# A graph layer on one core: the edge stage rebuilt, with 400 quads of 500 edges in place of 391 of 512

## The chip, the cores and the metric

The kernel runs on one core of a Trainium2 chip. The time is the device time of one execution in microseconds (us); the median of three runs of the kernel before is 2057.42 us (2057.03 to 2058.61).

## The reference

12500 nodes of 64 features, 200000 edges sorted by their destination `dst`. All is float32.

```python
h = jnp.maximum(_layernorm(x, axis=-1), 0.0)
e = jnp.concatenate([h[src], h[dst]], axis=1)
m = jax.nn.relu(e @ W1 + b1) @ W2 + b2            # 128 -> 128 -> 64
s = jax.ops.segment_sum(m, dst, num_segments=n_nodes)
cnt = jax.ops.segment_sum(jnp.ones((m.shape[0],)), dst, num_segments=n_nodes)
return x + s / jnp.maximum(cnt, 1.0)[:, None]
```

## The kernel before, in words

**Node stage.** The layer norm is worked out in ten groups of ten nodes for each of 125 partitions. PE multiplies h with the two halves of W1 (`products`, L815 to L819). The first half gives table P, the second, with b1 added by DVE (L659), table Q; both are stored in HBM by SP (L295, L296), in pieces of 112 and 13 partitions. So an edge needs relu(P[src] + Q[dst]).

**Edge tables.** `src` and `dst` are turned into columns by PE (L795): `src_e` holds the source of each edge as an integer, `rel_e` its destination less the smallest destination of its quad (L604).

**Edge stage.** A quad is 512 edges in four chunks of 128. There are 391 quads. As `dst` is sorted, the destinations of a quad lie in a window of 128 nodes if no quad's span is wider; `if_one_window` (L221) takes the branch `fast` then, as with this data. For quad n:

- ACT copies four columns of indices into `idx` (L484), nine quads ahead; POOL then issues four indirect DMAs, each of which fetches 128 rows of P into `g`, a ring of 12 quads (L388). The first 12 quads are gathered ahead of the loop.
- SP loads the window, 128 rows of Q, into `qw` (L307).
- DVE compares `rel_e` with the numbers 0 to 127, chunk by chunk: `member`, ones and zeros, edges by nodes (L675). ACT makes a bf16 copy (L514), PE transposes it (L894) and also counts with it (L899), ACT copies the transposes to `spread` (L490) and the counts to SBUF (L497).
- PE multiplies `spread` with the window (L874): Q[dst] of each edge. DVE adds the gathered rows (L685), ACT does the relu (L508).
- PE sums the edges of each node: `r` by `member` (L885). ACT copies the sums (L502), PE multiplies them with w2 and adds b2 times the counts (L905, L906), and DVE adds this to the window's columns of `acc` (L704) and the counts to `count` (L697).

The order on each engine is written out by hand: `quads(n)` works on different quads, PE's on the products of quad n-1, the sums of n-2, the transposes of n, the w2 product of n-3. `rounds` (L207) puts twelve such steps into a loop. Waits are on semaphores that count quads, with a credit of `RING` so that a value is never negative.

**Output.** SP fetches the counts laid out by node (L326), DVE takes their reciprocals (L709, L711). PE transposes `acc`, a node of each partition's hundred at a time (L975), and DVE (L785) or ACT and POOL (L573, L416) scale it and add x; SP stores. The 25 batches of four go through eight PSUM banks.

## Time and profile before

| | us |
|---|---|
| plain runs, median of 3 | 2057.4 |
| profiled execution, span from first to last instruction | 3104.2 |
| PE busy, matrix products | 1916.4 |
| POOL busy | 1516.6 |
| ACT busy | 884.8 |
| DVE busy | 866.9 |
| first gather starts at | 62.0 |
| output stage starts at | 3077.0 |

The profile is of one execution, and beside its span no separate time of that execution is given. Mind that the span is 1.5 times the plain runs. Busy time counts instructions that compute or generate descriptors; waiting isn't in it. PE's matrix products are pipelined, and a float32 product is recorded as two passes.

### The profile page before, as it was taken

How to read it: one execution, taken by the hardware profiler on the slowest of the kernel's cores; microseconds unless marked ns; L12 is line 12 of the kernel's file. 1: busy time of each engine (PE TensorE's matmuls, PEld its weight loads, DVE VectorE, ACT ScalarE, POOL GpSimd, SP SyncE). 2: the span in 40 equal slices, each digit the busy share in tenths (PEclk: the TensorE clock that was granted, in tenths of full speed). 3: DMA queues.
4: the chain of work that ended last, by engine and by line, in shares of the span. 5: the costliest groups of instructions: out<-in, count | busy, mean ns of one | idle time of the engine just before them, and what ended most of it. 6: DMA issues, size and time to landing. Idle time of an engine off the chain costs nothing.

```text
span 3104.2 us, 46493 instructions
## 1 busy us (share of the span) xinstructions
PE 1916.4 (62%) x11540; PEld 1632.1 (53%) x11541; DVE 866.9 (28%) x2889; ACT 884.8 (29%) x2458; POOL 1516.6 (49%) x1611
## 2 busy tenths in 40 slices
PE   6256555655655566765556665565655667665568
PEld 6255444545555555554445555454555556554457
DVE  6122222222222222222222222222222222222224
ACT  3123222322222222222222222222222222222224
POOL 5445444544545444454445444454545445454451
PEclk9577777777777776677777667777777766677778
DMA  6311111111111111111111111111111111111111
GB/s 183 92 52 46 43 44 43 43 43 44 44 43 45 43 43 43 44 45 43 44 43 46 43 44 43 43 45 44 44 44 44 44 43 44 44 44 44 44 44 43
DMA packets 112927, 150.93 MB, mean 49 GB/s; under 512 B 32653, under 2 KB 83212, under 8 KB 112750
## 3 DMA queue, kind: packets, MB, share of 16 engines
q0 software_dynamic: 50016, 102.53, 12.6%
q1 hardware_dynamic: 62170, 46.62, 5.1%
q14 instruction: 165, 1.35, 0.1%
q10 hardware_dynamic: 564, 0.23, 0.0%
q8 instruction: 12, 0.20, 0.0%
HBM read 133.09 MB, written 16.07 MB: 48 GB/s over the span
## 4 chain that ended last, share of the span: by engine, by line
another core or an unknown queue 41%; PE 28%; issue 14%; ACT 10%; DVE 4%; DVEq 2%; DMA 1%; ACTq 1%; SPq 0%; POOL 0%; PEldq 0%; POOLq 0%
PE bank L874 12%; PE bank L885 11%; ACT spread L490 4%; ACT member L514 3%; PE bank L894 2%; DVE z L685 2%; ACT spans_i L497 1%; DVEq L689 1%; PE bank L975 1%; PE bank L817 1%; ACT idx L484 1%; PE bank L905 1%; PE bank L899 0%; PE bank L906 0%
## 5 line engine op out<-in xcount | busy, mean ns | idle before, releaser
L388 POOL DMA_INDIRECT g<-p_table,idx x1563 | 1476.0, 944 | 1504.6 <-ACT idx L484 1022.8
L874 PE MATMUL bank<-qw,spread 128*128 128x128 f32 x3126 | 647.1, 371 | 1044.4 <-ACT spread L490 985.2
L874 PEld LDWEIGHTS bank<-qw,spread 128*128 128x128 f32 x3126 | 551.4, 265 | 1106.8 <-ACT spread L490 857.0
L490 ACT CAST spread<-bank 128x512 f32<-128x512 bf16 x391 | 228.7, 585 | 1713.2 <-remote 1335.2
L885 PE MATMUL bank<-member,r 128*128 128x128 f32 x3126 | 616.9, 360 | 63.3 <-DVE acc L704 42.5
L697 DVE TENSOR_TENSOR area<-area,spans_i 1x128 f32 x391 | 109.6, 280 | 1949.0 <-ACT spans_i L497 1773.9
L885 PEld LDWEIGHTS bank<-member,r 128*128 128x128 f32 x3126 | 544.8, 263 | 106.6 <-DVE acc L704 38.9
L675 DVE TENSOR_SCALAR member<-columns,rel_e 128x128 f32<-128x128 f32 x1563 | 349.2, 290 | 107.0 <-PE bank L885 85.2
L508 ACT ACTIVATE r<-z 128x512 f32<-128x512 f32 x391 | 246.1, 630 | 371.5 <-DVE z L685 279.5
L685 DVE TENSOR_TENSOR z<-bank,g 128x512 f32<-128x512 f32 x391 | 263.7, 674 | 0.0
L514 ACT CAST member<-member 128x512 bf16<-128x512 f32 x391 | 235.3, 602 | 4.3 <-DVE member L675 4.3
L905 PE MATMUL bank<-w 128*128 128x128 f32 x782 | 211.4, 356 | 0.0
L906 PE MATMUL bank<-spans_i,b_row 1*128 1x128 f32 x782 | 197.9, 334 | 0.0
L894 PE MATMUL bank<-ident,member 128*128 128x128 bf16 x1563 | 183.3, 251 | 5.1 <-issue 5.1
L899 PE MATMUL bank<-member,ones 128*1 128x128 bf16 x1563 | 172.9, 242 | 0.0
L905 PEld LDWEIGHTS bank<-w 128*128 128x128 f32 x782 | 131.6, 211 | 56.7 <-issue 23.6
L894 PEld LDWEIGHTS bank<-ident,member 128*128 128x128 bf16 x1563 | 149.2, 117 | 17.0 <-ACT member L514 5.3
L906 PEld LDWEIGHTS bank<-spans_i,b_row 1*128 1x128 f32 x782 | 120.7, 193 | 52.6 <-issue 11.9
L704 DVE TENSOR_TENSOR acc<-acc,bank 128x128 f32 x391 | 112.8, 289 | 81.5 <-issue 43.7
L899 PEld LDWEIGHTS bank<-member,ones 128*1 128x1 bf16 x1563 | 88.5, 88 | 52.2 <-issue 24.3
L497 ACT COPY spans_i<-bank 1x128 f32<-1x128 f32 x391 | 98.0, 251 | 4.2 <-remote 3.2
L502 ACT COPY w<-bank 128x128 f32<-128x128 f32 x391 | 97.5, 249 | 4.6 <-PE bank L885 4.6
(66 smaller groups left out, 434.8 us busy)
## 6 DMA issues: line engine op xcount, KB each, us to landing
qw<-q_table SPq DMA_DIRECT2D x391, 64.0 KB
g<-p_table,idx POOLq DMA_INDIRECT x1563
p_table<-area SPq DMA_DIRECT2D x10, 560.0 KB
q_table<-area SPq DMA_DIRECT2D x10, 560.0 KB
xs<-in_x_dram SPq DMA_DIRECT2D x5, 560.0 KB
out_dram<-xs SPq DMA_DIRECT2D x3, 672.0 KB
acc<-in_src_dram SPq DMA_DIRECT2D x1, 768.0 KB
acc<-in_dst_dram SPq DMA_DIRECT2D x1, 768.0 KB
```

The source lines that it names most:

```text
L388: nc.gpsimd.indirect_dma_start(out=g[:, k, j * HID:(j + 1) * HID], out_offset=None, in_=p_table, in_offset=bass.IndirectOffsetOnAxis(ap=id ...
L490: nc.scalar.copy(spread[:, k % 2, :, :].rearrange("p c e -> p (c e)")[:, 0:w], t_bank[k % 2][:, 0:w]).then_inc(spread_done, 1)
L508: nc.scalar.activation(r[:, k % 2, 0:w], z[:, k % 2, 0:w], ACT.Relu).then_inc(r_done, 1)
L514: nc.scalar.copy(member16[:, k % MEMBERS, 0:c, :], member[:, k % MEMBERS, 0:c, :]).then_inc(member16_done, 1)
L675: last = nc.vector.tensor_scalar(member[:, k % MEMBERS, j, :], columns[:, :], rel_e[:, bass.ds(n * 4 + j, 1)], None, ALU.is_equal)
L685: nc.vector.tensor_tensor(z[:, k % 2, 0:w], z_bank[k % 2][:, 0:w], g[:, k, 0:w], ALU.add).then_inc(z_done, 1)
L874: last = nc.tensor.matmul(z_bank[k % 2][:, HID * j:HID * (j + 1)], spread[:, k % 2, j, :], qw[:, k, :], start=True, stop=True)
L885: last = nc.tensor.matmul(sums[:, 0:WIN], r[:, k % 2, HID * c:HID * (c + 1)], member[:, k % MEMBERS, c, :], start=c == 0, stop=c == chunks ...
L894: last = nc.tensor.transpose(t_bank[k % 2][:, 128 * c:128 * (c + 1)], member16[:, k % MEMBERS, c, :], ident16[:, :])
L899: last = nc.tensor.matmul(c_bank[k % 2][0:1, 0:WIN], ones16[:, :], member16[:, k % MEMBERS, c, :], start=c == 0, stop=c == chunks_of(n) - 1)
L905: nc.tensor.matmul(u_bank[k][:, 2 * WIN:3 * WIN], w2[:, :], of_sums, start=True, stop=False)
L906: return nc.tensor.matmul(u_bank[k][:, 2 * WIN:3 * WIN], b2_row[:, :], of_counts, start=False, stop=True)
```

## The change

- A quad is 500 edges, four chunks of 125; there are 400 quads, none partly filled. 1600 gathers of 125 rows replace 1563 of 128. They read their indices from `src_e`; `idx` is gone. The ring has 16 quads, the windows a ring of their own of 8.
- The transposed membership is made in another way: `rel_q` holds the relative destinations of a quad in one row, as bf16 (values over 255 cut to 255). PE spreads that row over 128 partitions with a product (`broadcast_rows`), and DVE compares it with each partition's number (`spread_of`). `member` is made by one comparison of the quad; the counts use its upper halves as bf16.
- The sum z and its relu are written in place in `g`.
- What is added to `acc` is the sum of the relu rows, straight from PSUM, and the counts too. The products with w2 and b2 are made at the end for all nodes, in place of the transposes of `acc`.
- The loops are written out without `Fori`.

The diff, cut to its core:

```diff
-QE = 512
+ROWS = 125
+QE = 4 * ROWS
-RING = 12
+RING = 16
+WINDOWS = 8
+FAR = 255.0
-MEMBERS = 4
+MEMBERS = 3
...
+        def ones_and_zeros(k, c):
+            return member[0:ROWS, k, c, :].bitcast(BF16).rearrange("e (w h) -> e w h", h=2)[:, :, 1]
...
             def fast():
-                rounds(sp, 0, QUADS, load_window)
+                for n in range(QUADS):
+                    k = n % WINDOWS
+                    if n >= WINDOWS:
+                        sp.wait_ge(zq_done, n - WINDOWS + 1)
+                    at = sp.value_load(base_i[0:1, n:n + 1], min_val=0, max_val=NODES - 1)
+                    sp.dma_start(qw[:, k, :], q_table[bass.ds(at, WIN), :]).then_inc(window_in[k], 16)
...
-            def gather(n, k, use):
-                ready = pool.to_reg(n + 1)
-                pool.wait_ge(p_out[0], all_out[0])
-                pool.wait_ge(idx_ready, ready)
+            pool.wait_ge(src_table, QT)
+            def gather(n):
+                k = n % RING
+                if n >= RING:
+                    pool.wait_ge(u_psum, n - RING + 1)
                 for j in range(chunks_of(n)):
                     nc.gpsimd.indirect_dma_start(
-                        out=g[:, k, j * HID:(j + 1) * HID], out_offset=None, in_=p_table,
-                        in_offset=bass.IndirectOffsetOnAxis(ap=idx[:, k, j:j + 1], axis=0)).then_inc(gathered[k], 16)
+                        out=g[0:ROWS, k, j * HID:(j + 1) * HID], out_offset=None, in_=p_table,
+                        in_offset=bass.IndirectOffsetOnAxis(ap=src_e[0:ROWS, 4 * n + j:4 * n + j + 1], axis=0))\
+                        .then_inc(gathered[k], 16)
...
             def fast():
-                for n in range(LAG):
-                    quads(n, n, 0)
-                rounds(act, LAG, QUADS - LEAD, quads)
...
+                for n in range(QUADS):
+                    w = HID * chunks_of(n)
+                    act.wait_ge(z_done, n + 1)
+                    nc.scalar.activation(g[0:ROWS, n % RING, 0:w], g[0:ROWS, n % RING, 0:w], ACT.Relu)\
+                        .then_inc(r_done, 1)
...
+            def rows_of():
+                dve.wait_ge(low_done, 1)
+                for t in range(QT):
+                    nc.vector.tensor_scalar(rel_q[:, t, :], dst_f[:, t, :], low[:, t:t + 1], FAR,
+                                            ALU.subtract, ALU.min).then_inc(row_table, 1)
...
+            def spread_of(n):
+                w = ROWS * chunks_of(n)
+                dve.wait_ge(row_done, n + 1)
+                if n >= 2:
+                    dve.wait_ge(zq_done, n - 1)
+                nc.vector.tensor_scalar(spread[:, n % 2, 0:w], row_bank[n % 2][:, 0:w], rows_f[:, :], None,
+                                        ALU.is_equal).then_inc(spread_done, 1)
+            def members_of(n):
+                if n >= MEMBERS:
+                    dve.wait_ge(u_psum, n - MEMBERS + 1)
+                nc.vector.tensor_tensor(member[0:ROWS, n % MEMBERS, :, :],
+                                        columns[0:ROWS, :].unsqueeze(1).to_broadcast([ROWS, 4, WIN]),
+                                        rel_e[0:ROWS, 4 * n:4 * n + 4].unsqueeze(2).to_broadcast([ROWS, 4, WIN]),
+                                        ALU.is_equal).then_inc(member_done, 1)
+            def add_rows(n):
                 w = HID * chunks_of(n)
+                rows_n = g[0:ROWS, n % RING, 0:w]
+                dve.wait_ge(zq_done, n + 1)
+                dve.wait_ge(gathered[n % RING], n // RING * 64 + 16 * chunks_of(n))
+                nc.vector.tensor_tensor(rows_n, z_bank[n % 2][0:ROWS, 0:w], rows_n, ALU.add).then_inc(z_done, 1)
+            def add_sums(n):
+                at = dve.value_load(base_i[0:1, n:n + 1], min_val=0, max_val=NODES - 1)
+                v, c = acc[:, bass.ds(at, WIN)], count[:, bass.ds(at, WIN)]
+                dve.wait_ge(u_psum, n + 1)
...
+                nc.vector.tensor_tensor(v, v, u_bank[n % 2][:, 0:WIN], ALU.add).then_inc(v_done, 1)
...
+                nc.vector.tensor_tensor(c, c, u_bank[n % 2][0:1, WIN:2 * WIN], ALU.add).then_inc(c_done, 1)
...
+                for n in range(QUADS + 2):
+                    if n + 1 < QUADS:
+                        spread_of(n + 1)
+                    if n < QUADS:
+                        add_rows(n)
+                    if n + 1 < QUADS:
+                        members_of(n + 1)
+                    if n >= 2:
+                        add_sums(n - 2)
...
+            def broadcast_rows(n):
+                w = ROWS * chunks_of(n)
+                if n >= 2:
+                    pe.wait_ge(spread_done, n - 1)
+                nc.tensor.matmul(row_bank[n % 2][:, 0:w], ident16[:, n % 128:n % 128 + 1].to_broadcast([128, 128]),
+                                 rel_q[:, n // 128, 0:w], start=True, stop=True).then_inc(row_done, 1)
+            def spread_q(n):
...
+                for c in range(chunks_of(n)):
+                    last = nc.tensor.matmul(z_bank[n % 2][0:ROWS, HID * c:HID * (c + 1)], chunk(spread, n % 2, c),
+                                            qw[:, n % WINDOWS, :], start=True, stop=True)
...
+            def sum_rows(to, rows_n, k, chunks):
                 for c in range(chunks):
+                    nc.tensor.matmul(to[0:1, WIN:2 * WIN], ones16[0:ROWS, :], ones_and_zeros(k, c),
+                                     start=c == 0, stop=c == chunks - 1)
+                for c in range(chunks):
+                    last = nc.tensor.matmul(to[:, 0:WIN], rows_n[:, HID * c:HID * (c + 1)], member[0:ROWS, k, c, :],
+                                            start=c == 0, stop=c == chunks - 1)
+                return last
...
+                broadcast_rows(0)
+                for n in range(QUADS + 1):
+                    if n + 1 < QUADS:
+                        broadcast_rows(n + 1)
+                    if n < QUADS:
+                        spread_q(n)
+                    if n >= 1:
+                        sum_edges(n - 1)
...
                 for t in range(BT):
                     node = slice(BT * b + t, BT * b + t + (NP - 1) * NT + 1, NT)
-                    last = nc.tensor.transpose(bank[b % 8][0:NP, 128 * t:128 * (t + 1)], acc[:, node], ident[:, :])
+                    to = bank[b % 8][0:NP, 128 * t:128 * t + FEAT]
+                    nc.tensor.matmul(to, acc[:, node], w2[:, :], start=True, stop=False)
+                    last = nc.tensor.matmul(to, count[:, node], b2_row[:, :], start=False, stop=True)
                 last.then_inc(o_psum, 1)
```

## Rows read from the trace of the kernel before

**Rows 1.** The page: the span, and the busy time of each engine.

```profile
span 3104.2 us, 46493 instructions
PE 1916.4 (62%) x11540; PEld 1632.1 (53%) x11541; DVE 866.9 (28%) x2889; ACT 884.8 (29%) x2458; POOL 1516.6 (49%) x1611
```

**Rows 2.** Waits in total: engine, line, releaser: us in total, times, longest us.

```profile
POOL g L388 <- ACT idx L484: 1022.8, 192, 37.8
PE bank L874 <- ACT spread L490: 985.2, 174, 6.9
```

**Rows 3.** Timeline of POOL in the loop: start, us, what, idle before and its releaser.

```profile
1509.26 0.94 POOL L388 DMA_INDIRECT g<-p_table,idx  x1 [0.30 <-issue]
1515.25 0.94 POOL L388 DMA_INDIRECT g<-p_table,idx  x1 [5.04 <-ACT idx L484]
```

**Rows 4.** Timeline of DVE ahead of the loop.

```profile
121.97 1.62 DVE L659 TENSOR_TENSOR area<-bank,b_all 125x512 f32<-125x512 f32 x3 [44.52 <-issue]
```

**Rows 5.** Timeline of POOL, its first 48 gathers.

```profile
62.00 1.14 POOL L388 DMA_INDIRECT g<-p_table,idx  x1 [17.96 <-DMA p_table<-area]
63.45 0.95 POOL L388 DMA_INDIRECT g<-p_table,idx  x1 [0.31 <-issue]
...
119.62 0.94 POOL L388 DMA_INDIRECT g<-p_table,idx  x1 [0.30 <-issue]
```

**Rows 6.** Timeline from the last quad to the output stage.

```profile
3067.41 0.90 SPq L326 DMA_DIRECT2D b_all<-area  x1
...
3068.12 0.56 DVE L685 TENSOR_TENSOR z<-bank,g 128x384 f32<-128x384 f32 x1
...
3071.32 0.21 DVE L709 TENSOR_SCALAR mean<-b_all 125x100 f32<-125x100 f32 x1 [2.65 <-DMA b_all<-area]
...
3077.01 23.22 PE L975 MATMUL bank<-ident,acc 128*125 128x128 f32 x100 [0.70 <-DVE acc L704]
```

**Rows 7.** Timeline of PE near the end, all gathers issued.

```profile
3040.12 1.16 PE L874 MATMUL bank<-qw,spread 128*128 128x128 f32 x8
...
3042.86 0.38 PE L899 MATMUL bank<-member,ones 128*1 128x128 bf16 x4
...
3044.00 1.16 PE L874 MATMUL bank<-qw,spread 128*128 128x128 f32 x8
```

**Rows 8.** Busy us by stretch: PE, PEld, DVE, ACT, POOL; granted clock, DMA share, GB/s.

```profile
3040.00:3064.00 24.00, 22.44 (x175) 18.32 (x175) 12.36 (x43) 12.15 (x30) 0.00 (x0) 1.00 0.01 1
1512.30:1517.40 5.10, 5.08 (x26) 4.55 (x26) 1.98 (x7) 2.17 (x7) 1.84 (x2) 0.52 0.09 26
```

**Rows 9.** Groups of instructions: line, what, count; busy, mean ns; idle before.

```profile
L388 POOL DMA_INDIRECT g<-p_table,idx x1563 | 1476.0, 944 | 1504.6 <-ACT idx L484 1022.8 <-issue 463.8 <-DMA p_table<-area 18.0
...
L675 DVE TENSOR_SCALAR member<-columns,rel_e 128x128 f32<-128x128 f32 x1563 | 349.2, 290 | 107.0 <-PE bank L885 85.2 <-issue 20.1 <-PEq L866 0.7
L685 DVE TENSOR_TENSOR z<-bank,g 128x512 f32<-128x512 f32 x391 | 263.7, 674 | 0.0
L508 ACT ACTIVATE r<-z 128x512 f32<-128x512 f32 x391 | 246.1, 630 | 371.5 <-DVE z L685 279.5 <-issue 92.0
...
L697 DVE TENSOR_TENSOR area<-area,spans_i 1x128 f32 x391 | 109.6, 280 | 1949.0 <-ACT spans_i L497 1773.9 <-issue 169.2 <-DMA area<-spread 5.9
...
L604 DVE TENSOR_TENSOR rel_e<-bank,base 128x512 f32<-128x512 f32 x4 | 4.3, 1076 | 8.0 <-remote 8.0
```

**Rows 10.** Timeline of PE in the products for table Q.

```profile
132.24 10.21 PE L817 MATMUL bank<-w,area 128*125 128x128 f32 x80 [0.30 <-DVE area L659]
```

**Rows 11.** Timeline of SP's queue, two stores of table Q.

```profile
132.21 0.32 SPq L295 DMA_DIRECT2D q_table<-area  x1
...
132.57 0.40 SPq L296 DMA_DIRECT2D q_table<-area  x1
```

**Rows 12.** DMA queues: packets, MB, share of 16 engines.

```profile
q0 software_dynamic: 50016, 102.53, 12.6%
```

**Rows 13.** Timeline of PE in the loop, at the lower granted clock.

```profile
1512.32 2.05 PE L874 MATMUL bank<-qw,spread 128*128 128x128 f32 x8 [6.58 <-ACT spread L490]
```

355 lines of the change are left out of this document (93 added, 262 removed).

## The prediction, made before the change was run

> **What bounds the kernel now.** I read the page's span and busy line first [rows 1]. No engine is full, and the profiled execution is half as long again as the plain runs: 3104.2 us of span against a median of 2057.4 us. So its span can't be split up as it stands; first it has to be seen what the plain runs do without. The waits in total say it [rows 2]: POOL waited 1022.8 us for the index copy of ACT, and PE 985.2 us for ACT's `spread`. The difference between the two times is 1046.8 us, nearly POOL's wait alone. In POOL's timeline [rows 3] gathers come in blocks of eight with a hole of 5 to 6 us between blocks. And ahead of the loop DVE stood for 44.52 us waiting for products of PE, and went on at 121.97 us, just when POOL's first 48 gathers were out [rows 4]: in the profiled execution PE hardly moves while gathers are issued. Had the plain runs this too, they would not end at 2057 us. So I take the holes for a cost of being profiled.
>
> What is left is a floor. The first gather starts at 62.00 us [rows 5], once table P is written. From the one at 63.45 to the one at 119.62 there are 45 steps of 1.248 us: 0.94 of work and 0.30 to the next. 1563 of them are 1950.6 us, and the first took 0.2 longer. At the end, from the addition of the last quad at 3068.12 us to the end of the span, there are 36.1 us [rows 6]. The sum is 62.0 + 0.2 + 1950.6 + 36.1 = 2048.9 us. The median is 2057.4, so 8.5 us remain for the landing of the last gather and for what lies around the span. **POOL issues gathers without a pause from 62 us to about 2013 us, and that sets the time.** The rest of the edge stage is faster: near the end, with all gathers issued, a quad took 3.87 us [rows 7] at a granted clock of 1.00 [rows 8], against 4 x 1.248 = 4.99 us for its gathers.
>
> All sums below go from the plain median by differences, since the profiled span is not comparable.
>
> **Part 1, 1600 gathers in place of 1563.** POOL issues four for each of 400 quads. What one costs with 125 rows no row shows: every gather of the trace has 128, and takes 944 ns in the mean [rows 9]. If the price belongs to the instruction: 37 x 1.248 = +46.2 us. If all of the 0.944 belongs to the rows, it becomes 0.922, the step 1.226, and 1600 of them take 1961.6 us: +11 us. Nothing excludes less or more than these; the rivals take that up. I take +46, since the 0.30 us gap surely goes by instruction and nothing shows that the rest does not. The index now comes straight from `src_e`: the wait on ACT goes, but in the plain runs there is none by the argument above, so 0.
>
> **Part 2, what is taken off PE, ACT and DVE.** Per quad go the four transposes, the w2 and b2 products, four ACT copies (L490, L497, L502, L514) and the index copy. In come one bf16 product of 500 columns, a comparison of DVE out of PSUM (`spread_of`), and one comparison of 512 elements (`members_of`) for four of 128. PE per quad: two groups of eight passes at 1.16 us, the count products 0.38, and the broadcast, as many columns as those four, again some 0.38: 3.1 us against 3.87 [rows 7]. DVE: the addition 0.67, the two comparisons at most 0.67 and 1.08 (the strided L604), two sums at 0.28: 3.0 us [rows 9]. ACT has one relu, 0.63 us. All lie below 4.99 us, so the saving is worth 0 in the loop; POOL hides it. If that cover went, some 3.1 to 3.5 us a quad would be next. A ring of 16 quads and 8 windows loaded some 30 us ahead leave SP's and POOL's waits with slack: gather n now waits for the sums of quad n - 16, long done. `rows_of` puts four comparisons of some 0.7 us on DVE ahead of the Q products; 64 gathers issued ahead, 80 us against 60 before, cover them.
>
> **Part 3, the end.** Before, from the last addition at 3068.12 to PE's first transpose at 3077.01 it is 8.9 us [rows 6], through ACT's copies and the w2 product. After: addition 0.67, relu 0.63, counts 0.38, sums 1.16, two DVE sums 0.56 [rows 7, 9], and some 0.7 for five hand-overs (an estimate): 4.1 us, so -4.8 us. The counts, early before, now end with the last quad. Their DMA took from 3067.41 to 3071.32, and with the two scale steps it is some 5 us behind the last sum; PE fills eight banks meanwhile, so this is hidden. Without that cover it is +5. Then PE does w2 and b2 for all nodes: for 100 transposes in 23.22 us [rows 6] come 200 products of two passes, 400 passes. The nearest row has 128 moving columns: 80 passes in 10.21 us, 0.128 us each [rows 10], which would make 51 us. These have 64 columns, and the four bf16 passes above took 0.38 us, 0.095 each. I take 0.09: 36 us, +13 us, with +1 (0.06) and +28 as ends.
>
> **Sum.** 2057.4 + 46.2 - 4.8 + 13 = 2111.8, say 2112 us, 2.7% slower. Its bounds give 2057.4 + 11 - 4.8 + 1 = 2065 to 2057.4 + 46.2 + 28 = 2132, and with 1% more on the step (20 us) some 2150.
>
> **Rivals.**
> 1. *A gather of 125 rows is dearer, chance 0.17.* 125 is no multiple of 16, so its rows can't be shared out evenly over the 16 DMA engines as 128 can. The nearest rows: on SP the store of 112 rows took 0.32 us to issue, that of 13 rows 0.40 [rows 11]. With 0.08 us more per gather it is 1600 x 0.08 = +128, so 2240 us; with a quarter more on 0.944, 1600 x 0.236 = +378, so 2490 us. That the gathers were all alike speaks neither for nor against. On the DMA's side it would not matter: the packets of q0 took 12.6% of 16 engines over the span [rows 12], 6258 us, 4.0 us of one engine per gather; on five engines that is 0.8 us, below the step of 1.25. The Trainium skill (DMA: Bandwidth & Descriptors, "Why a DMA increments its semaphore by 16 and not by 1") says that a DMA is given the largest number of engines up to 16 that divides its slowest dimension, which makes 5 of 125; no run here shows it.
> 2. *It is cheaper, chance 0.16 (the other side).* If part of the 0.944 us goes by engines served and fewer are served, the step shrinks on POOL, the one place that sets the time. It decides from 2111.8 - 2057.4 = 54.4 us over 1600 gathers, 0.034 us: a step under 1.214. If a third of 0.944 went by 16 engines and five were left, 0.315 x 11/16 = 0.216 us less, it would be 2112 - 346 = 1766 us. With still more gone the loop would hang on PE and DVE: 62 + 400 x 3.5 + 53 = 1515 us. Against it: a gather's fixed part may be all of it.
> 3. *DVE gets in POOL's way, chance 0.04.* `members_of` has two inputs in SBUF. Were a gather to stand for all of its 0.67 us, 400 x 0.67 = +268, so 2380 us. Against it: L697 adds two SBUF operands 391 times and L675 runs 1563 times in the loop, and the mean of all gathers is 944 ns [rows 9], as where DVE rested [rows 5]. By the rows it costs a gather nothing. The Trainium skill (SBUF — State Buffer, "Who interferes with whom") holds that such a DVE instruction contends with a GpSimd one that reads SBUF, which these rows don't show.
> 4. *PE at its lower clock becomes the pace, chance 0.03.* At a granted clock of 0.52 [rows 8] a group of eight passes took 2.05 us [rows 13]; with two of them and some 1.1 for the rest, 5.2 us a quad, 0.2 over POOL: +84, so 2196 us. PE would then be busy all the time, and after such work the clock was seen at 1.00.
>
> **Chances.** The forecast has 0.58; the 0.02 that is left is for any other gain. A measurement of this kernel can tell about 0.2%, 4 us, from no change. The forecast's own range, 2065 to 2150, lies on the slower side. With its and the rivals' parts near zero: faster 0.18, same 0.04, slower 0.78. To leave out no more than 2 in 10, the range reaches from 2058, for small gains of the step, to 2290, over rival 4 and the lower part of rival 1.
>
> **What would show it.** In the profile after: 1600 DMA_INDIRECT with a mean near 944 ns, at steps of 1.25 us where nothing is waited for. A mean of 0.90 or less is rival 2, of 1.02 or more rival 1, or 3 where the long ones lie beside `members_of`. The output stage should take some 36 us on PE, PE's groups of a quad 3.1 us. The profiled execution may again be long for its own reasons; then the steps within the blocks count, not the span. The number is wrong outside 2058 to 2290, and the reasoning is wrong if a profile whose span is near its plain time shows POOL resting between gathers.

## The result, and the profile after

The changed kernel takes 2671.97 us (median of 4 runs, 2671.18 to 2674.49), the kernel before beside it 2058.02 us (4 runs, 2057.03 to 2059.72). The ratio is 1.2985, with a 95% interval of 1.2967 to 1.3003: 614 us more, where 54 were forecast.

The page of the changed kernel, its span, its busy line and POOL's DMA queue:

```profile
span 2670.6 us, 29512 instructions
...
PE 1776.6 (67%) x9298; PEld 1546.9 (58%) x9299; DVE 1007.5 (38%) x2157; ACT 301.0 (11%) x512; POOL 2020.4 (76%) x1647
...
q0 software_dynamic: 128000, 104.26, 16.8%
```

Here the span is the plain time less 1.4 us, unlike before [rows 1]. POOL is the fullest engine, at 76%. The queue q0 carries 128000 packets, 80 for each of the 1600 gathers; before it was 50016, or 32 for each of 1563 [rows 12].

The groups of instructions of the changed kernel (line, what, count; busy, mean ns; idle before and its releasers):

```profile
L375 POOL DMA_INDIRECT g<-p_table,src_e x1600 | 1980.1, 1238 | 505.4 <-issue 472.1
L609 DVE TENSOR_TENSOR g<-bank,g 125x512 f32<-125x512 f32 x400 | 276.8, 692 | 1505.5 <-DMA g<-p_table,src_e 1427.4
...
L599 DVE TENSOR_TENSOR member<-columns,rel_e 125x512 f32<-125x512 f32 x400 | 272.6, 682 | 0.0
...
L855 PE MATMUL bank<-w,acc 128*125 128x64 f32 x200 | 72.0, 462 | 1.1 <-DVE area L620 1.1
L856 PE MATMUL bank<-b_row,area 1*125 1x64 f32 x200 | 71.3, 457 | 0.0
```

A gather takes 1238 ns in the mean, against 944 before [rows 9]. Its idle time is `issue`, the 0.30 us between one and the next, and little else. DVE waits for gathers: POOL is what the loop hangs on. Now comes POOL's timeline at the first gathers (start, us, what, idle before and its releaser):

```profile
62.72 1.40 POOL L375 DMA_INDIRECT g<-p_table,src_e  x1 [18.02 <-DMA p_table<-area]
64.42 1.21 POOL L375 DMA_INDIRECT g<-p_table,src_e  x1 [0.31 <-issue]
65.93 1.21 POOL L375 DMA_INDIRECT g<-p_table,src_e  x1 [0.30 <-issue]
```

The step is 1.51 us where it was 1.248 [rows 5], with the same 0.30 between two. Here DVE does no work of the loop yet and at most one gather is under way, so the 1.21 is the gather's own. In the loop, all engines, the same view shows one thing more:

```profile
1502.32 1.21 POOL L375 DMA_INDIRECT g<-p_table,src_e  x1 [0.31 <-issue]
1502.71 0.69 DVE L609 TENSOR_TENSOR g<-bank,g 125x512 f32<-125x512 f32 x1 [3.79 <-DMA g<-p_table,src_e]
1503.32 0.68 DVE L599 TENSOR_TENSOR member<-columns,rel_e 125x512 f32<-125x512 f32 x1
...
1503.83 1.25 POOL L375 DMA_INDIRECT g<-p_table,src_e  x1 [0.30 <-issue]
...
1505.39 1.21 POOL L375 DMA_INDIRECT g<-p_table,src_e  x1 [0.30 <-issue]
```

The gather that starts while DVE makes `member` is longer than its neighbours. It is nearly always the third of a quad: over the 1536 gathers behind the first 64, taken by their place in the quad, the third has a mean of 1.324 us and the other three 1.209. Nowhere in the loop does POOL rest over 1 us between two gathers.

The end, same view:

```profile
2529.00 1.21 POOL L375 DMA_INDIRECT g<-p_table,src_e  x1 [0.30 <-issue]
...
2532.43 0.69 DVE L609 TENSOR_TENSOR g<-bank,g 125x512 f32<-125x512 f32 x1 [4.43 <-DMA g<-p_table,src_e]
...
2537.32 0.90 SPq L313 DMA_DIRECT2D b_all<-area  x1
...
2537.63 0.72 PE L855 MATMUL bank<-w,acc 128*125 128x64 f32 x2 [1.15 <-DVE area L620]
...
2538.28 0.71 PE L856 MATMUL bank<-b_row,area 1*125 1x64 f32 x2
...
2541.17 0.21 DVE L625 TENSOR_SCALAR mean<-b_all 125x100 f32<-125x100 f32 x1 [4.07 <-DMA b_all<-area]
```

A product of two passes begins every 0.65 us, 0.323 us a pass, and there are 400 passes: 129 us, against 23.2 for the transposes before [rows 6]. The stretch in the view by windows (us; PE, PEld, DVE, ACT, POOL busy; granted clock, DMA share, GB/s):

```profile
2540.00:2660.00 120.00, 120.00 (x373) 98.39 (x372) 11.31 (x50) 10.19 (x44) 8.00 (x11) 0.50 0.08 24
```

PE is busy all the time, and the granted clock is 0.50, its level of 1.2 GHz. PEld is PE's loading of weights, which runs beside its products. In the stretch near the end of the kernel before, the clock was 1.00 [rows 8].

**The account.** The first gather starts 0.7 us later (62.72 for 62.00). From there to the end of the last gather at 2530.2 us it is 2467.5, against 1950.8 by the sum of the prediction: +516.7. From the last addition to the end of the span it is 138.2 against 36.1: +102.1. What remains, the landing of the last gather and what lies around the span, is 2.2 + 1.4 = 3.6 us, against 2058.0 - 2048.9 = 9.1: -5.5. Together +614.0. The gathers' +516.7 divide into 37 more at the old step, 46; 1600 times 1.209 less 0.944, 424; and 400 times the 0.114 of the third, 46. So four things are to be explained: the price, the third gather, the output stage's pass, and, as it turned out, the kernel before itself.

### The profile page after: what moved, and what is told of

It reads as the page before. It is cut to its first block, busy times and chain, and to the rows that moved or that the text cites. A ratio compares the mean times of both kernels' runs of the same rounds, so it can differ in the third digit from the quotient of the medians.

```text
span 2670.6 us, 29512 instructions
## 1 busy us (share of the span) xinstructions
PE 1776.6 (67%) x9298; PEld 1546.9 (58%) x9299; DVE 1007.5 (38%) x2157; ACT 301.0 (11%) x512; POOL 2020.4 (76%) x1647
## 3 DMA queue, kind: packets, MB, share of 16 engines
q0 software_dynamic: 128000, 104.26, 16.8%
q8 instruction: 76, 1.25, 0.2%
## 4 chain that ended last, share of the span: by engine, by line
POOL 64%; issue 17%; PE 10%; DMA 6%; DVE 2%; DVEq 1%; ACT 0%; SPq 0%; POOLq 0%
POOL g L375 64%; DMA g<-p_table,src_e 6%; PE bank L799 3%; PE bank L855 2%; PE bank L856 2%; PE bank L727 1%; PE bank L796 1%; DVE g L609 1%; DVE acc L617 0%; DMA xs<-in_x_dram 0%; DVE area L620 0%; DVEq L612 0%; PE bank L720 0%; DVE area L511 0%; DMA p_table<-area 0%
## 5 line engine op out<-in xcount | busy, mean ns | idle before, releaser
L375 POOL DMA_INDIRECT g<-p_table,src_e x1600 | 1980.1, 1238 | 505.4 <-issue 472.1
L609 DVE TENSOR_TENSOR g<-bank,g 125x512 f32<-125x512 f32 x400 | 276.8, 692 | 1505.5 <-DMA g<-p_table,src_e 1427.4
L790 PEld LDWEIGHTS bank<-qw,spread 128*125 128x125 f32 x3200 | 672.5, 290 | 58.3 <-DVE spread L593 9.1
L799 PE MATMUL bank<-member,g 125*128 125x128 f32 x3200 | 696.7, 386 | 0.0
L790 PE MATMUL bank<-qw,spread 128*125 128x128 f32 x3200 | 652.7, 373 | 8.3 <-DMA qw<-q_table 8.3
L799 PEld LDWEIGHTS bank<-member,g 125*128 125x128 f32 x3200 | 588.9, 275 | 66.0 <-issue 40.4
L466 ACT ACTIVATE g<-g 125x512 f32<-125x512 f32 x400 | 251.9, 630 | 2197.7 <-DVE g L609 2197.7
L593 DVE TENSOR_SCALAR spread<-bank,rows_f 128x500 f32<-128x500 f32 x400 | 288.2, 720 | 10.2 <-DMA area<-spread 9.6
L599 DVE TENSOR_TENSOR member<-columns,rel_e 125x512 f32<-125x512 f32 x400 | 272.6, 682 | 0.0
L781 PE MATMUL bank<-rel_q,ident 128*128 128x500 bf16 x400 | 230.3, 576 | 5.7 <-issue 5.7
```

The source lines that it names most:

```text
L375: nc.gpsimd.indirect_dma_start(out=g[0:ROWS, k, j * HID:(j + 1) * HID], out_offset=None, in_=p_table, in_offset=bass.IndirectOffsetOnAxis( ...
L466: nc.scalar.activation(g[0:ROWS, n % RING, 0:w], g[0:ROWS, n % RING, 0:w], ACT.Relu)\
L593: nc.vector.tensor_scalar(spread[:, n % 2, 0:w], row_bank[n % 2][:, 0:w], rows_f[:, :], None, ALU.is_equal).then_inc(spread_done, 1)
L599: nc.vector.tensor_tensor(member[0:ROWS, n % MEMBERS, :, :], columns[0:ROWS, :].unsqueeze(1).to_broadcast([ROWS, 4, WIN]), rel_e[0:ROWS, 4 ...
L609: nc.vector.tensor_tensor(rows_n, z_bank[n % 2][0:ROWS, 0:w], rows_n, ALU.add).then_inc(z_done, 1)
L781: nc.tensor.matmul(row_bank[n % 2][:, 0:w], ident16[:, n % 128:n % 128 + 1].to_broadcast([128, 128]), rel_q[:, n // 128, 0:w], start=True, ...
```

## Experiments

### What a gather costs, by its number of rows

**mix_rows**: the kernel before, each of the twelve quads of the ring with a row count of its own. The remaining rows of `g` keep what was in them; `g` is zeroed at the start, as also in before_125, before_112 and before_126.

```diff
+            counts = (128, 127, 126, 125, 124, 120, 113, 112, 96, 64, 32, 16)
...
+                rows_n = counts[k]
...
-                        out=g[:, k, j * HID:(j + 1) * HID], out_offset=None, in_=p_table,
-                        in_offset=bass.IndirectOffsetOnAxis(ap=idx[:, k, j:j + 1], axis=0)).then_inc(gathered[k], 16)
+                        out=g[0:rows_n, k, j * HID:(j + 1) * HID], out_offset=None, in_=p_table,
+                        in_offset=bass.IndirectOffsetOnAxis(ap=idx[0:rows_n, k, j:j + 1], axis=0)).then_inc(gathered[k], 16)
```

> The kernel before, with the four gathers of each of the twelve ring places cut to 128, 127, 126, 125, 124, 120, 113, 112, 96, 64, 32 and 16 rows (the rest of an edge chunk gets rows of zeros or old ones; part of the sum is left out). Theory A, a gather is dear when its rows can't be shared out evenly over 16 DMA engines: 128, 112, 96, 64, 32 and 16 rows at 0.94 us or less, 125 rows at 1.21 us as in the changed kernel, 127 and 113 (primes) at least as dear, 120 (fifteen engines of eight) near 1.0. Theory B, the 1.21 us comes from the index being read in place from the wide table, or from the loops written out: 125 rows as cheap as 128 here, 0.94 us. Theory C, the price goes by rows alone: 16 rows far below 0.94, all others between in proportion.

Measured: 2512.16 us (one run). POOL's timeline, one gather of each of eight counts (113, 112, 16, 128, 127, 126, 125 and 124 rows, in this order):

```profile
1504.19 2.36 POOL L394 DMA_INDIRECT g<-p_table,idx  x1 [0.30 <-issue]
...
1514.86 0.93 POOL L394 DMA_INDIRECT g<-p_table,idx  x1 [0.30 <-issue]
...
1535.32 0.84 POOL L394 DMA_INDIRECT g<-p_table,idx  x1 [0.30 <-issue]
...
1542.54 0.94 POOL L394 DMA_INDIRECT g<-p_table,idx  x1 [0.30 <-issue]
...
1546.72 2.55 POOL L394 DMA_INDIRECT g<-p_table,idx  x1 [0.31 <-issue]
...
1556.61 0.99 POOL L394 DMA_INDIRECT g<-p_table,idx  x1 [0.30 <-issue]
...
1561.96 1.20 POOL L394 DMA_INDIRECT g<-p_table,idx  x1 [0.30 <-issue]
...
1568.04 1.29 POOL L394 DMA_INDIRECT g<-p_table,idx  x1 [0.30 <-issue]
```

113 rows cost 2.36 us and 112 rows 0.93. So it is no matter of the number of rows, and not of being a multiple of 16 either: 126 rows, at 0.99, cost little more than 128. What orders the twelve is the largest divisor of the count up to 16. The means over the whole run, with that divisor k and the rows of one share, count / k:

```
rows      128   127   126   125   124   120   113   112    96    64    32    16
k          16     1    14     5     4    15     1    16    16    16    16    16
rows / k    8   127     9    25    31     8   113     7     6     4     2     1
mean us  0.96  2.56  0.98  1.19  1.29  0.99  2.36  0.93  0.91  0.90  0.87  0.85
```

A straight line through its two ends, 0.85 us and 0.0136 for every further row of a share, passes all the others within 0.05 us. For 125 rows it gives 0.85 + 24 x 0.0136 = 1.18; the mean was 1.19 here, 1.21 in the changed kernel.

**after_128**: the changed kernel, with gathers of 128 rows into the same buffers (rows 125 to 127 fetch row 0 of P and are not used).

```diff
...
-                        out=g[0:ROWS, k, j * HID:(j + 1) * HID], out_offset=None, in_=p_table,
-                        in_offset=bass.IndirectOffsetOnAxis(ap=src_e[0:ROWS, 4 * n + j:4 * n + j + 1], axis=0))\
+                        out=g[:, k, j * HID:(j + 1) * HID], out_offset=None, in_=p_table,
+                        in_offset=bass.IndirectOffsetOnAxis(ap=src_e[:, 4 * n + j:4 * n + j + 1], axis=0))\
```

> The changed kernel, its 1600 gathers made 128 rows long (three rows more than are used, index 0). Theory A (uneven sharing): a gather back at 0.944 us, 0.265 us less, 1600 times: 2672 - 424 = 2248 us. Theory B (index from the wide table, or written-out code): 1.21 us and 2672 us as before.

Measured: 2230.13 us (2227.72 to 2231.53), ratio 1.0842 (1.0824 to 1.0860), 442 us below the change with the same number of gathers. Its group of gathers:

```profile
L377 POOL DMA_INDIRECT g<-p_table,src_e x1600 | 1534.0, 959 | 507.3 <-issue 433.6
```

1980.1 - 1534.0 = 446 us less for POOL, and the time fell by as much. It came out 18 us below what was expected, since the third gather of a quad is lengthened by 0.060 us here and not by 0.114; why is told below. **Three rows more in each gather take 72% of the loss away.**

**before_125**: the same step taken alone in the kernel before: 1563 gathers of 125 rows, nothing else changed.

```diff
...
-                        out=g[:, k, j * HID:(j + 1) * HID], out_offset=None, in_=p_table,
-                        in_offset=bass.IndirectOffsetOnAxis(ap=idx[:, k, j:j + 1], axis=0)).then_inc(gathered[k], 16)
+                        out=g[0:125, k, j * HID:(j + 1) * HID], out_offset=None, in_=p_table,
+                        in_offset=bass.IndirectOffsetOnAxis(ap=idx[0:125, k, j:j + 1], axis=0)).then_inc(gathered[k], 16)
```

> The kernel before with nothing changed but its gathers, each cut from 128 to 125 rows (three edges of each chunk get rows of zeros, so part of the sum is left out); still 1563 of them. Theory A (five engines for 125 rows, 1.19 us as in mix_rows, a step of 1.50): 2058 + 1563 x 0.25 = 2449 us. Rival (part of the loss in the loop came from the rebuilt stage, not from the row count): clearly less, down to 2058 us.

Measured: 2474.33 us (2473.33 to 2475.05). The group:

```profile
L391 POOL DMA_INDIRECT g<-p_table,idx x1563 | 1896.4, 1213 | 494.5 <-issue 475.9
```

1213 ns, in the old loop, where no comparison with two operands in SBUF runs for a whole quad. With its step of 1.517 us, the prediction's floor gives 2057.4 + 1563 x (1.517 - 1.248) = 2478: so the kernel as it was pays the same price. The expected 2449 had taken the 1.19 of mix_rows for a gather. But on this chip the kernel before took 3054.62 us, not 2058, and the ratio was 0.8114 (0.8063 to 0.8165). Of that more below.

### The third gather of a quad

**after_tt**: the changed kernel, with the comparison that makes `spread` as a `tensor_tensor`, to see whether that form is what lengthens a gather.

```diff
-                nc.vector.tensor_scalar(spread[:, n % 2, 0:w], row_bank[n % 2][:, 0:w], rows_f[:, :], None,
-                                        ALU.is_equal).then_inc(spread_done, 1)
+                nc.vector.tensor_tensor(spread[:, n % 2, 0:w], row_bank[n % 2][:, 0:w],
+                                        rows_f[:, 0:1].to_broadcast([128, w]), ALU.is_equal).then_inc(spread_done, 1)
```

> The changed kernel with the comparison that makes spread done as a tensor-tensor operation with a broadcast operand instead of a tensor-scalar one. Of the 1600 gathers some 390 that lie beside it take 1.32 us instead of 1.21. Theory L (the tensor-scalar form locks GpSimd out of its port): these fall to 1.21 us, 400 x 0.115 = 46 us less, 2626 us. Rival M (another DVE operation beside them does it, the member comparison or the two sums): they stay, 2672 us.

Measured: 2670.55 us (2669.17 to 2674.00), ratio 1.2986 (1.2965 to 1.3008), the change's own time; the third gather still has a mean of 1.313 us. So `spread` is not what holds it up.

**rebuilt_512**: the change's loop with quads of 512 edges: 391 quads, 1563 gathers of 128.

```diff
-ROWS = 125
+ROWS = 128
```

> The changed kernel with chunks of 128 edges: 391 quads of 512, 1563 gathers of 128 rows. Theory A: 62.7 + 1563 x 1.248 + 391 x 0.115 for the lengthened ones + 2 + 138 for the end + 1.4 outside the span = 2200 us. Theory B: 62.7 + 1563 x 1.533 + 141 = 2600 us. If the rebuilt stage with fewer operations gained anything in the loop, it would end below 2200 us.

Measured: 2184.05 us (2180.56 to 2184.86), ratio 1.0611 (1.0593 to 1.0628). POOL and DVE in its timeline:

```profile
1503.89 1.00 POOL L375 DMA_INDIRECT g<-p_table,src_e  x1 [0.30 <-issue]
```

```profile
1503.39 0.68 DVE L599 TENSOR_TENSOR member<-columns,rel_e 128x512 f32<-128x512 f32 x1
```

The third gather is again the longer one, a mean of 1.009 us against 0.944 of the others. **members_ts** is this kernel with `member` made by four comparisons, each with one tile and one scalar per partition:

```diff
-                nc.vector.tensor_tensor(member[0:ROWS, n % MEMBERS, :, :],
-                                        columns[0:ROWS, :].unsqueeze(1).to_broadcast([ROWS, 4, WIN]),
-                                        rel_e[0:ROWS, 4 * n:4 * n + 4].unsqueeze(2).to_broadcast([ROWS, 4, WIN]),
-                                        ALU.is_equal).then_inc(member_done, 1)
+                for c in range(4):
+                    last = nc.vector.tensor_scalar(member[0:ROWS, n % MEMBERS, c, :], columns[0:ROWS, :],
+                                                   rel_e[0:ROWS, 4 * n + c:4 * n + c + 1], None, ALU.is_equal)
+                last.then_inc(member_done, 1)
```

> rebuilt_512 with member made by four tensor-scalar comparisons, as in the kernel before, in place of one tensor-tensor comparison with two operands in SBUF. In rebuilt_512 the third gather of each quad, which starts while that comparison runs, takes 1.009 us in the mean, the others 0.943. Theory N (the two-operand comparison holds up the gather's reading of its indices): the third falls to 0.944 too, 391 x 0.066 = 26 us less, 2184 - 26 = 2158 us. Rival (something else in that place, the sums added to acc and count, or the landing of a window): it stays near 1.01 us and 2184 us.

```profile
L375 POOL DMA_INDIRECT g<-p_table,src_e x1563 | 1481.4, 948 | 833.7 <-issue 419.3
```

The third gather fell to 0.946 us, the mean of all to 948 ns: the comparison with two operands in SBUF is what lengthens it. The time gives no verdict on what that saves: 2533.35 us, on the chip where the kernel before took 3054.62, with 187 gaps of over 1 us between gathers, 394 us in all. **r512_again** and **ts_again**, the same two kernels on one chip, were to settle it.

> rebuilt_512 once more, beside the kernel before. That kernel took 2058 us on one chip and 3055 us on another. Where it takes 2058 us here: 2184 us again. Where it takes 3055 us: Theory H (on such a chip the other engines are held up while gathers of 128 rows are issued back to back): near the 2533 us of members_ts. Rival (members_ts was slow by its own comparisons of DVE): 2184 us there too.

> members_ts once more. Where the kernel before takes 2058 us: 26 us below rebuilt_512, 2158 us, since its third gathers took 0.946 us; the rival (the tensor-scalar comparisons cause holes of their own) says 2533 us on this chip too. Where it takes 3055 us: 2533 us.

Measured: 2554.22 us (2552.86 to 2555.12) and 2558.07 us (2557.38 to 2560.57), where the kernel before took 3100.52. The mean gather is 977 ns in the first and 946 in the second, 48 us of POOL's work, and yet the second is no faster: it has 188 gaps with 423 us, the first 126 with 354. Here, what POOL saved came back as gaps. That members_ts would save time on the first kind of chip was not measured.

In r512_again it is not the third gather that is long but the second, with a mean of 1.074 us against 0.944 of the others, though the kernel is that of rebuilt_512. One of them:

```profile
1500.11 0.68 DVE L599 TENSOR_TENSOR member<-columns,rel_e 128x512 f32<-128x512 f32 x1
1500.29 1.32 POOL L375 DMA_INDIRECT g<-p_table,src_e  x1 [0.31 <-issue]
```

The comparison ends at 1500.79, 0.50 us after the gather began, and the gather takes 0.38 us more than 0.94. In the line of rebuilt_512 above 0.18 us of it were left, and the gather took 0.06 more; in that of the change 0.17 were left, and it took 0.04 more. The records of whole runs give one rule. A gather that starts with more than 0.15 us of that comparison still to run is longer than the median by what is left of it, less 0.127 us: in all 364 such cases of the change (125 rows) and in all 143 of r512_again (128 rows), with a standard deviation of 0.003 us. The longest took 0.46 and 0.48 us more. A gather that is already under way when the comparison starts isn't lengthened. In rebuilt_512 three gathers began within 0.02 us of it, and there it was the comparison that took longer, 0.73 to 0.74 us. So the number of rows has no part in this, nor has the place in the quad: what counts is how late in the comparison a gather begins, 0.24 us before its end in the mean in the change.

### The output stage

All of these are to tell what makes its pass 0.323 us long. **out_nob2** is the changed kernel with 200 passes in place of 400, **out_contig** has the columns of `acc` in another order, one next to the other:

```diff
-                    nc.tensor.matmul(to, acc[:, node], w2[:, :], start=True, stop=False)
-                    last = nc.tensor.matmul(to, count[:, node], b2_row[:, :], start=False, stop=True)
+                    last = nc.tensor.matmul(to, acc[:, node], w2[:, :], start=True, stop=True)
```

```diff
-                    node = slice(BT * b + t, BT * b + t + (NP - 1) * NT + 1, NT)
+                    node = slice(NP * (BT * b + t), NP * (BT * b + t + 1))
```

> The changed kernel without the b2 products of the output stage (b2 times the counts is left out), 200 passes in place of 400 there. Theory Q (each pass has a fixed price of 0.32 us, whatever it multiplies): the stage halves, 129 to 65 us, 2672 - 65 = 2607 us, clock at 0.50 as now. Rival P (the one-partition products keep the granted clock at 0.50): the clock rises towards 1.00 and the 200 passes take 25 to 46 us, so below 2590 us.

> The changed kernel with the columns of acc and count in the output stage taken next to each other instead of 100 apart (the sums of other nodes are used, which changes the result). Theory S (the step of 400 bytes in the weights sets the 0.32 us of a pass): a pass falls towards the 0.13 us of the table products, 129 to 50 us or so, 2672 - 75 = 2597 us. Rival Q (number and kind of passes at the low clock): it stays at 2672 us.

Measured: out_nob2 2585.71 us (2583.11 to 2586.66), 86 us below the change's 2671.97, which is another chip's, but, as a run below shows, one that doesn't depend on the chip; out_contig 2663.21 (2661.69 to 2664.11), 9 us below it. With the b2 products between, the stride is worth 0.02 us a pass (0.303 for 0.323), so it is not what makes that 0.323. The groups of out_nob2, and its stretch at this point:

```profile
L855 PE MATMUL bank<-w,acc 128*125 128x64 f32 x200 | 46.1, 435 | 1.1 <-DVE area L620 1.1
L855 PEld LDWEIGHTS bank<-w,acc 128*125 128x125 f32 x200 | 45.9, 326 | 1.4 <-issue 1.4
```

```profile
2555.00:2570.00 15.00, 15.00 (x68) 15.00 (x67) 3.46 (x17) 3.71 (x16) 3.11 (x5) 0.50 0.32 102
```

46.1 / 200 = 0.231 us a pass. The time came out below the 2607 us that equal passes would give, on the side of Rival P, but not by way of the clock: that stayed at 0.50. So neither holds as it was put. Two more, both on rebuilt_512, separate what is left. **out_twice** keeps 400 passes, all of them with `acc` as weights; **out_wide** has 200 passes, with w2 filled up with zeros to 128 columns.

```diff
-                    last = nc.tensor.matmul(to, count[:, node], b2_row[:, :], start=False, stop=True)
+                    last = nc.tensor.matmul(to, acc[:, node], w2[:, :], start=False, stop=True)
```

```diff
-        w2 = sb("w2", [HID, FEAT])
+        w2 = sb("w2", [HID, 128])
...
-                    nc.tensor.matmul(to, acc[:, node], w2[:, :], start=True, stop=False)
-                    last = nc.tensor.matmul(to, count[:, node], b2_row[:, :], start=False, stop=True)
+                    last = nc.tensor.matmul(bank[b % 8][0:NP, 128 * t:128 * (t + 1)], acc[:, node], w2[:, :],
+                                            start=True, stop=True)
```

> rebuilt_512 with the b2 product of the output stage replaced by a second w2 product (the result has w2 twice and no b2), still 400 passes. A pass took 0.323 us with the b2 products between, 0.231 without them. Theory R (the one-partition product between the others costs the extra): 400 x 0.231 = 92 us, 129 - 92 = 37 us less than rebuilt_512. Rival (adding a second product to the same place in PSUM costs it): 129 us, no change against rebuilt_512.

> rebuilt_512 without the b2 product and with w2 widened by zeros to 128 columns, 200 passes. out_nob2 had 64 columns, a granted clock of 0.50 all through the stage, and 0.231 us a pass. Theory W (columns drive the clock): the clock rises towards 1.00 as in the transposes of the kernel before (0.93, 128 columns, 0.232 us), and the pass stays 0.23 us, since the weights with a step of 400 bytes set it: 46 us for the stage, 83 us less than rebuilt_512. Rival (the clock stays at 0.50): a pass gets longer, 0.3 us or more, 60 us for the stage.

Measured, against r512_again of the same chip (2554.22): out_twice 2517.41 us (2515.84 to 2519.64), -36.8; out_wide 2471.23 us (2469.72 to 2472.42), -83.0. Stretches of the output stage, first of out_twice, then of out_wide, and the group of the latter:

```profile
2430.00:2510.00 80.00, 79.32 (x346) 79.13 (x345) 10.10 (x48) 9.30 (x40) 7.28 (x10) 0.50 0.12 37
```

```profile
2430.00:2440.00 10.00, 10.00 (x45) 10.00 (x45) 2.19 (x11) 2.78 (x12) 2.18 (x3) 1.00 0.24 77
```

```profile
L856 PE MATMUL bank<-w,acc 128*125 128x128 f32 x200 | 46.2, 397 | 1.0 <-DVE area L621 1.0
```

In out_wide, with 128 moving columns, the clock is 1.00 in this stretch, and a pass takes 46.2 / 200 = 0.231 us; in out_nob2, with 64 columns at a clock of 0.50, it takes the same. PEld is as busy as PE in both, which fits a pace set by the loading of `acc` as weights; no run changed that load alone. The products with one row of b2 between them, which load weights for one partition, add the rest: 400 x (0.323 - 0.231) = 37 us. So the stage's 106 us more are 300 passes more than the 100 transposes at 0.231, 69 us, and 37 for the b2 products.

Two things stay open. Why a pass costs 0.092 us more with b2 products between: it may be the alternation or the one-partition products themselves, and no run had them at the higher clock. And what makes the load 0.231 us, when table Q's passes took 0.128 [rows 10]. The stride remains the nearest candidate: table Q's weights lie one next to the other, those of `acc` 400 bytes apart. Between the two passes of one product PEld's loads began 0.207 us apart in the change and 0.162 in out_contig. Columns next to each other without the b2 products between, which would decide it, were not run.

### The kernel before on other chips

**after_again** is the changed kernel unaltered. It ran on another chip than the experiments so far, and so did the other three of this part.

> The changed kernel itself, once more, for where the kernel before takes 3050 to 3100 us. Theory H (the other engines are held up there only while gathers of 128 rows follow each other every 1.25 us; those of 125 rows come every 1.51): 2672 us as on the first chip, so faster than the kernel before there. Rival: it is held up too, well over 2672 us. Where the kernel before takes 2058 us: 2672 us, slower by 30%.

Measured: 2673.77 us (2672.83 to 2675.86), and the kernel before 3048.27 us (10 runs, 3032.06 to 3059.55): ratio 0.8772 (0.8742 to 0.8801). **The change is 30% slower on one chip and 12% faster on another, and its own time is the same on both.** (The record doesn't name the chip of the first result; but after_tt, with the change's time, ran on one where the kernel before took 2057.72 us.) What differs is the kernel before. Its plain runs of 3030 us and more were not profiled, so how long each engine waits in them isn't shown. But in every other trace here the span is 1.8 to 2.3 us below the time of that same execution, and the trace of the kernel before, with its span of 3104.2 us, has the mark of a slow chip. This is the same stretch, all with gathers being issued, of rebuilt_512, of r512_again, of the kernel before and of after_again (the columns as in the windows above):

```profile
110.00:120.00 10.00, 9.95 (x84) 8.95 (x84) 9.47 (x20) 2.52 (x4) 7.62 (x8) 1.00 0.31 81
110.00:120.00 10.00, 0.00 (x0) 0.00 (x0) 0.00 (x0) 0.00 (x0) 7.56 (x9) 0.50 0.20 52
110.00:120.00 10.00, 0.00 (x0) 0.00 (x0) 0.00 (x0) 0.00 (x0) 7.56 (x9) 0.50 0.20 52
110.00:120.00 10.00, 9.26 (x79) 8.18 (x77) 7.61 (x16) 1.89 (x3) 7.87 (x8) 1.00 0.30 78
```

The first two are one and the same kernel: PE works for 9.95 of 10 us on the one chip and not at all on the other, with POOL alike. The kernel before shows the second picture, and the change, on a chip of that kind, the first. So the holes in the trace of before [rows 3] are most likely real ones. Its 214 gaps of over 1 us sum up to 1051 us. The times of rebuilt_512 differ likewise, 2184 us and 2554; one of its gaps, in the timeline of r512_again:

```profile
1513.15 0.94 POOL L375 DMA_INDIRECT g<-p_table,src_e  x1 [0.31 <-issue]
1516.66 0.94 POOL L375 DMA_INDIRECT g<-p_table,src_e  x1 [2.57 <-PE bank L799]
```

The group of after_again shows why it is spared; it has no such gap:

```profile
L375 POOL DMA_INDIRECT g<-p_table,src_e x1600 | 1978.0, 1236 | 507.6 <-issue 473.4
```

Is it the pace of the gathers, or how they are shared out? **before_112** and **before_126** are before_125 with other counts:

```diff
-                        out=g[0:125, k, j * HID:(j + 1) * HID], out_offset=None, in_=p_table,
-                        in_offset=bass.IndirectOffsetOnAxis(ap=idx[0:125, k, j:j + 1], axis=0)).then_inc(gathered[k], 16)
+                        out=g[0:112, k, j * HID:(j + 1) * HID], out_offset=None, in_=p_table,
+                        in_offset=bass.IndirectOffsetOnAxis(ap=idx[0:112, k, j:j + 1], axis=0)).then_inc(gathered[k], 16)
```

> The kernel before with 112 rows in each gather (16 edges of each chunk get rows of zeros): sixteen engines, 0.928 us and a step of 1.23. Where the kernel before takes 2058 us: 2058 - 1563 x 0.016 = 2033 us. Where it takes 3055 us or more: held up as well, about as long (Theory H, and by either of its reasons, pace or sixteen engines); if only full gathers of 128 rows did it, 2033 us.

> The kernel before with 126 rows in each gather: fourteen engines, 0.98 us and a step of 1.284. Where the kernel before takes 2058 us: 2058 + 1563 x 0.036 = 2114 us. Where it takes 3055 us or more: if the pace of the gathers holds the others up, still far above 2114 us; if the use of all sixteen engines does, 2114 us.

Measured: before_112 3115.6 us (two runs, 3114.97 and 3116.23), ratio 1.0218; before_126 3069.54 us (3065.11 to 3076.70), ratio 1.0068 (1.0041 to 1.0095). The waits in total of before_112:

```profile
POOL g L391 <- ACT idx L487: 1078.1, 190, 37.6
```

Fewer rows don't remove the gaps, and neither does a count whose divisor is 14: before_126 has 190 gaps with 957 us. What the kernels with gaps have in common is a step of 1.24 to 1.30 us; those with 125 rows have 1.51. **r512_paced** puts a small memset and a wait for it ahead of every gather of rebuilt_512:

```diff
+                    nc.gpsimd.memset(idle[:, :], 0.0).then_inc(paced, 1)
+                    pool.wait_ge(paced, 4 * n + j + 1)
                     nc.gpsimd.indirect_dma_start(
```

> rebuilt_512 with a small memset and a wait for it ahead of each gather on POOL, which makes the step some 0.15 us longer. Where the kernel before takes 2058 us: 2184 + 1563 x 0.15 = 2418 us. Where it takes 3055 us or more, rebuilt_512 took 2554 us: if the pace holds the others up, the holes go or shrink and it ends near 2420 us in spite of more work on POOL; if the sixteen engines do, the holes stay and it takes 2554 us or more.

Measured: 2536.62 us (2534.47 to 2538.28). Its timeline:

```profile
1503.51 0.95 POOL L379 DMA_INDIRECT g<-p_table,src_e  x1 [0.27 <-issue]
1504.46 0.14 POOL L377 MEMSET idle<- 128x32 f32 x1
1504.87 0.95 POOL L379 DMA_INDIRECT g<-p_table,src_e  x1 [0.27 <-issue]
```

The step is 1.36 us, and the gaps of over 1 us fell from 126 with 354 us (r512_again, on another chip of this kind) to 69 with 120 us. Without the gaps, the mean from one gather to the next is 1.41 us there against 1.28 in r512_again, which makes some 200 us more for POOL; the kernel still ended 18 us earlier. That difference proves little, since the kernel before took 52 us less on this chip. The gaps say more: the pace matters, but at 1.36 us they are fewer, not gone, and the time of about 2420 us for a loop without them was missed.

What the chips differ in, and what in them is late, is open. Each chip was used at one time only, so a condition of that hour is not told apart from the chip. The records show semaphores that arrive late at several engines at once, not which path delays them.

## Why the prediction was wrong

**What sets the time.** "POOL issues gathers without a pause from 62 us to about 2013 us, and that sets the time." For the chip of the forecast this held. The change's profile, whose span is its plain time, shows POOL from 62.72 to 2530.2 us with no pause, and rebuilt_512, with everything taken off PE, ACT and DVE, gained nothing there: 2184.05 - 2057.72 = 126 us, which are the 25 us of its third gathers (391 x 0.065) and the 102 of the end. **The argument beside it failed**: "I take the holes for a cost of being profiled". Plain runs took over 3030 us on three chips, and no profiled execution on the first kind of chip has a hole. The floor was right, since 2057 us can't hold them, but the span of the same trace was the kernel's time elsewhere, and there the change, whose gathers are slow enough, wins. The sign depends on the chip, and no case of the forecast had that.

**Part 1, the step that failed.** "I take +46, since the 0.30 us gap surely goes by instruction and nothing shows that the rest does not." The 37 more gathers did cost 46 us, and the 0.30 did stay. The 0.944 did not: it became 1.209, +424 us, outside both bounds of that part (+11 and +46). The one bound kept the price by instruction, the other scaled it with the rows, as if 125 were nearly 128; neither let 125 rows cost more. The mechanism stood as rival 1, with 0.17, and was priced by a quarter on 0.944, 0.236 us a gather; measured were 0.265 (28%), and with the third gather and the end the time lies above its 2490 us. On the DMA's side it had estimated 0.8 us a gather on five engines; by the 16.8% of q0 it is 0.9, below the step of 1.51. The cost is in the length of POOL's own instruction, which the second gather of all shows already; what POOL does in it no row tells. The Trainium skill (DMA: Bandwidth & Descriptors, "Why a DMA increments its semaphore by 16 and not by 1") has the rule that the largest divisor up to 16 sets the number of engines. In mix_rows the prices of all twelve counts go by that divisor, the dear ones being those of 127, 113, 124 and 125 rows. The prediction had the divisor 5 before it, and only a row of the trace was missing. That should have weighed for more than 0.17. Rival 2, that fewer engines are cheaper for POOL, is the reverse of what was measured: of two counts of nearly the same size, the one with fewer engines by that rule cost more.

**Part 2, the loop's cover.** Right where POOL is without holes: the work taken away was worth 0. The wait on ACT for the index copy counts only where the holes are.

**Rival 3, in part right.** "By the rows it costs a gather nothing" was read from a mean, and a mean hid it. `member` made with two operands in SBUF costs the gather that starts beside it 0.114 us in the change and 0.065 in rebuilt_512, 46 and 25 us in all, and members_ts shows the cause: 1.009 to 0.946 us. The gather does stand for nearly all of the comparison that is left, as the rival had it; that it costs a sixth of the 0.67 is a matter of when it starts. In the trace of before, L697 lasts 0.28 us, and only five gathers began with more than 0.13 us of it left. Four of them took 0.02 to 0.07 us more, much as by that rule; in the fifth case the addition itself took 0.36 us. The Trainium skill (SBUF — State Buffer, "Who interferes with whom") says that a DVE instruction with two SBUF inputs contends with a GpSimd one that reads SBUF; the runs agree.

**Part 3, the second term that failed.** The chain from the last addition to the output stage was put at 4.1 us and took 5.2 (2532.43 to 2537.63), so -3.7 for -4.8. The counts' DMA was hidden, as said: DVE had the counts at 2541.17 us, while PE went on. But "I take 0.09: 36 us" took 0.323: 129 us. The price came from rows with other weights [rows 7, 10]. The row of this very stage lay beside them: 100 transposes, with the same slices of `acc` as weights, in 23.22 us [rows 6], 0.232 us a pass. That alone would have given 400 x 0.232 = 93 us. The prediction used this row only as the thing to take away. The rest, 36 us, comes with the b2 products between, which no row of before shows.

**Rival 4.** PE's clock did fall, to a mean of 0.69 in the loop and 0.50 in the output stage. PE took about 4.0 us a quad (128.4 of each 200 us, 6.17 us a quad) for the predicted 3.1, still below its gathers, so it did not set the loop's pace. In the output stage a pass without b2 took 0.231 us at either level; whether the lower clock has a part in the 0.323 is open.

**A version that beats both.** On the chip where the kernel before takes 2058 us none was found: a gather as written here fetches one row for each of 128 partitions, so there are at least 1563, and 62 + 1951 + 36 us stand (argued from the rows, not run). Where it takes over 3030 us, every other kernel run there, but for those with 112 and 126 rows, is faster: rebuilt_512 with 2554 us and r512_paced with 2537, both doing the whole work, also beat the change's 2674.

## What to carry to other kernels

Choose the rows of an indirect DMA by their largest divisor up to 16, not by how well they divide the data: 128, 120, 112 or 126 rows cost POOL 0.93 to 0.99 us, 125 cost 1.2, 113 or 127 over 2.3. Price a moved or multiplied PE pass from a row with the same weights, and ask first whether PEld or PE sets its pace. Look where a gather starts beside a DVE instruction with two operands in SBUF: a mean over all gathers doesn't show it. And where a profile's span is far above the plain time, find out on a second chip which of the two is the kernel's time before calling the difference an artefact.

## What the runs showed of the hardware

- The time of an indirect DMA on POOL follows the rows divided by the largest divisor up to 16: 0.85 us and 0.0136 us for each further row of such a share, within 0.05 us for twelve row counts from 16 to 128 (mix_rows), with 0.30 us between two.
- A gather that starts beside a DVE comparison of 0.68 us with two operands in SBUF is lengthened by what is left of the comparison less 0.127 us, with 125 rows (the change) and with 128 (r512_again) alike; in the mean 0.115 and 0.30 us for the gathers that start within one. With one tile and one scalar per partition, the gathers of all four places took 0.946 us (ts_again).
- Fast gathers have gaps on some chips and none on others: the kernel before took 2058 us on two occasions and 3048, 3055 and 3101 us on three chips at other times, while the change took 2672 and 2674. At steps of 1.24 to 1.30 us the kernel before and its variants had 957 to 1078 us of gaps. There rebuilt_512 had 354 us of them at 1.25 and 120 us at 1.36, and kernels at 1.51 had none.
- PE, busy without pause and with the slices of `acc` as weights, took 0.231 us a pass at a granted clock of 0.50 (out_nob2, out_twice) and at 1.00 (out_wide).
